# A GRU in front of an RK4 network: the GRU's input products made in one go in fp32 ahead of the first step

## The reference

```python
def cell(h, x):                       # layer 0, GRU; initial h = cond
    gi = x @ W_ih + b_ih              # the input products
    gh = h @ W_hh + b_hh
    i_r, i_z, i_n = jnp.split(gi, 3, axis=-1)
    h_r, h_z, h_n = jnp.split(gh, 3, axis=-1)
    r = jax.nn.sigmoid(i_r + h_r)
    z = jax.nn.sigmoid(i_z + h_z)
    n = jnp.tanh(i_n + r * h_n)
    h_new = (1.0 - z) * n + z * h
    return (h_new, h_new)
...
def _derivative(q, p, drive, coupling, bias):     # layer 1, four times a step
    i_couple = jnp.tanh(q) @ coupling.T
    dq = q - q ** 3 / 3.0 - p + drive + i_couple + bias
    dp = EPSILON * (q + ALPHA - BETA * p)
    return (dq, dp)
...
x = x + gru(cond, x, ...)
x = x + rk4(cond, cond, x, ...)
x = x + attention_norm(x, ...)
x = x + resample(x, cond)
```

## Time and profile before

| what | value |
|---|---|
| time, median of 3 runs (lowest, highest) | 3905.99 us (3901.99, 3906.72) |
| the profiled execution's own time | 3899.93 us |
| its span (first to last instruction) | 3897.7 us |
| busy PE / DVE / POOL / ACT | 3572.1 / 3071.1 / 2305.7 / 1730.2 us |
| instructions | 307,384 |
| granted PE clock, mean | 0.984 |

### The profile page before, as it was taken

One profiled execution on the slowest core, in us unless ns is written; L12 is line 12 of the kernel. 1 busy time (PEld: TensorE's weight loads), 2 busy tenths in 40 slices (PEclk: granted clock), 3 DMA queues, 4 the chain that ended last, 5 costly groups with the idle time before them and its releaser, 6 DMA issues.

```text
span 3897.7 us, 307384 instructions
## 1 busy us (share of the span) xinstructions
PE 3572.1 (92%) x127757; PEld 3388.6 (87%) x127757; DVE 3071.1 (79%) x19466; ACT 1730.2 (44%) x14974; POOL 2305.7 (59%) x8762
## 2 busy tenths in 40 slices
PE   3999989999999999999999999999999999999987
PEld 3999988899898988999988998899999999899963
DVE  7877877777787877877777787788877778777876
ACT  3444444444444444444444444444444444444443
POOL 0666656666666666666666666666666666666642
PEclk7999999999999999999999999999999999999998
DMA  4000000000000000000000000000000000000001
GB/s 163 5 5 5 5 5 5 5 5 5 5 6 5 5 5 5 5 5 5 5 5 5 5 5 5 5 5 5 6 5 5 5 5 5 5 5 5 6 4 43
DMA packets 9266, 39.61 MB, mean 10 GB/s; under 512 B 524, under 2 KB 568, under 8 KB 7736
## 3 DMA queue, kind: packets, MB, share of 16 engines
q1 hardware_dynamic: 7776, 19.92, 1.4%
q10 hardware_dynamic: 88, 0.02, 0.0%
HBM read 15.75 MB, written 4.19 MB: 5 GB/s over the span
## 4 chain that ended last, share of the span: by engine, by line
PE 67%; DVE 11%; issue 10%; ACT 7%; POOL 5%; DMA 1%; DVEq 0%; SPq 0%; ACTq 0%; POOLq 0%
PE psum L1115 34%; PE psum L1088 23%; PE psum L1073 9%; ACT tpart L514 3%; POOL term L401 2%; DVE psum L890 2%; POOL sums L405 2%; ACT tfull L516 2%; DVE gates L775 2%; DVE tpart L832 1%; PE psum L1220 1%; DVE gates L769 1%; ACT qhat L521 1%; DVE psum L878 1%; ACT rz L481 1%
## 5 line engine op out<-in xcount | busy, mean ns | idle before, releaser
L1115 PE MATMUL psum<-tpart,cpl 128*128 128x32 f16 x65536 | 2025.7, 176 | 99.6 <-issue 80.9
L1115 PEld LDWEIGHTS psum<-tpart,cpl 128*128 128x128 f16 x65536 | 1814.8, 96 | 170.0 <-issue 117.3
L1088 PE MATMUL psum<-hpart,whh 128*128 128x32 f16 x49344 | 1520.6, 176 | 72.7 <-issue 56.2
L1088 PEld LDWEIGHTS psum<-hpart,whh 128*128 128x128 f16 x49344 | 1372.2, 96 | 97.8 <-issue 83.8
L514 ACT ACTIVATE tpart<-psum 128x8 f16<-128x8 f32 x4096 | 703.7, 178 | 1179.8 <-DVE psum L890 1145.4
L890 DVE TENSOR_REDUCE psum<-psum 128x8 f32<-128x24 f32 x4096 | 726.2, 189 | 325.8 <-PE psum L1115 245.0
L832 DVE SCALAR_TENSOR_TENSOR tpart<-tfull,tpart 128x8 f16<-128x8 f32 x4098 | 717.1, 178 | 147.0 <-ACT tfull L516 11.6
L401 POOL TENSOR_TENSOR term<-coef,qhat 128x32 f32<-128x32 f32 (+1 forms) x1536 | 431.0, 281 | 552.4 <-ACT qhat L521 551.5
L516 ACT ACTIVATE tfull<-psum 128x8 f32<-128x8 f32 x4096 | 688.1, 175 | 0.0
L878 DVE SCALAR_TENSOR_TENSOR psum<-cub,sums 128x16 f32<-128x16 f32 x1536 | 309.6, 202 | 228.7 <-POOL sums L405 147.6
L405 POOL TENSOR_TENSOR sums<-sums,term 128x32 f32<-128x32 f32 (+1 forms) x1536 | 410.3, 267 | 120.3
(11 more groups left out here) (167 smaller groups left out, 3642.4 us busy)
## 6 DMA issues: line engine op xcount, KB each, us to landing
xrow<-in_x_dram SPq DMA_DIRECT2D x4, 1024.0 KB, 13.4
out_dram<-space SPq DMA_DIRECT2D x16, 256.0 KB, 2.0
space<-in_L_cond_W_hh_dram SPq DMA_DIRECT2D x1, 3072.0 KB, 10.5
wih<-in_L_cond_W_ih_dram SPq DMA_DIRECT2D x1, 3072.0 KB, 19.8
space<-in_L_cond_coupling_dram SPq DMA_DIRECT2D x1, 1024.0 KB, 12.6
xrow<-in_cond_dram SPq DMA_DIRECT2D x1, 1024.0 KB, 4.4
wih<-in_L_cond_Wk_dram SPq DMA_DIRECT2D x1, 1024.0 KB, 9.8
wih<-in_L_cond_Wo_dram SPq DMA_DIRECT2D x1, 1024.0 KB, 11.8
```

The lines of the kernel that those rows point to most:

```text
L1088: mm = pe.matmul(gate_out[part][:, :, :, col:col + B], whh[:, w, k, n * P:(n + 1) * P], copies_in(hpart[:, k, :, :]), start=(col == 0 and ...
L1115: mm = pe.matmul(stage_out[a][:, :, :, col:col + B], cpl[:, w, k, n * P:(n + 1) * P], copies_in(tpart[:, s % 2, k, :, :]), start=(col == 0 ...
```

## The change

The input products leave the steps. Ahead of the first step x is loaded by chunks of 128 time steps (all batches), transposed, and multiplied with the unsplit fp32 W_ih, 128 steps x 4 batches = 512 columns at a time: 4 chunks x 12 tiles x 4 feature groups = 192 fp32 matmuls into four PSUM banks. ACT adds the bias and writes them into `gi`, now 48 x 512 columns of `space`, which holds all 512 steps. The coupling is transposed within chunk 1, and PE waits there until DVE has split it. The split of x and W_ih, their scales, `xpart`, `wihp`, `gisum` and DVE's sums go away. UNROLL goes away; the last two steps have no GRU work. W_ih is loaded in three column parts, behind the first chunk of x and ahead of W_hh.

```diff
-        XC = UNROLL * B
-        xpart = sb("xpart", [P, 2, UNROLL * KB], fp16)
-        gisum = sb("gisum", [P, G3, XC])
-        gi = sb("gi", [P, G3, UNROLL, B])
+        space = sb("space", [P, 48 * D])
+        gi = space[:, :].rearrange("p (t n b) -> p t n b", n=G3, b=B)
...
+            load_x(0)
+            for j in range(3):
+                sp.dma_start(wih[:, :, j * D:(j + 1) * D],
+                             W_ih[:, j * D:(j + 1) * D].rearrange("(k p) n -> p k n", p=P)).then_inc(in_wih[j], 16)
             sp.dma_start(w_row, W_hh.rearrange("(k p) n -> p k n", p=P)).then_inc(in_whh, 16)
+            load_x(1)
             sp.dma_start(c_row, coupling.rearrange("(n p) k -> p n k", p=P)).then_inc(in_c, 16)
...
+            def keep_inputs(i, tiles):
+
+                for n in tiles:
+                    g = i * G3 + n
+                    act.wait_ge(gi_mm, g + 1)
+                    act.activation(gi[:, i * P:(i + 1) * P, n, :], gbank[g % 4].rearrange("p (t b) -> p t b", b=B),
+                                   ACT.Identity, bias=bias3[:, 2, n:n + 1]).then_inc(gi_ready, 1)
...
+            for i in range(CHUNKS):
+                if i == CHUNKS - 1:
+                    act.wait_ge(whh_ready, 1)
+                keep_inputs(i, range(0, 2 * K))
+                if i + 1 < CHUNKS:
+                    turn_x(i + 1)
+                keep_inputs(i, range(2 * K, G3))
+                if i == 0:
+                    act.wait_ge(scales_ready, 1)
+                    for k in range(K):
+                        act.activation(whh[:, 0, k, :], w_row[:, k, :], ACT.Identity, scale=scale[:, 0:1]).then_inc(w_hi, 1)
...
-            for b in range(B):
-                dve.wait_ge(xT_ready, K * (b + 1))
-                dve.tensor_reduce(amax[:, 4 + b:5 + b], xT[:, :, :, b], AX.XY, ALU.max,
-                                  apply_absolute_value=True).then_inc(amax_ready, 1)
...
+            dve.wait_ge(gi_ready, GROUPS)
             dve.tensor_copy(hn_base.rearrange("p (k b) -> p k b", b=B),
                             bias3[:, 3, 2 * K:3 * K].unsqueeze(2).broadcast_to([P, K, B])).then_inc(hn_base_ready, 1)
...
-                    if u == 0 and s == 1:
-                        sum_inputs(N, at(2 * UNROLL))
-                    if u == UNROLL - 1 and s == 1:
-                        sum_inputs(RZ, at(3 * UNROLL))
...
+            def input_products(i, tiles):
+
+                for n in tiles:
+                    g = i * G3 + n
+                    if i == 0 and n % K == 0:
+                        pe.wait_ge(in_wih[n // K], 16)
+                    if n == 0:
+                        pe.wait_ge(xT_ready, B * (i + 1))
+                    if g >= 4:
+                        pe.wait_ge(gi_ready, g - 3)
+                    for k in range(K):
+                        mm = pe.matmul(gbank[g % 4], wih[:, k, n * P:(n + 1) * P], xT[:, i * P:(i + 1) * P, k, :],
+                                       start=(k == 0), stop=(k == K - 1))
+                    mm.then_inc(gi_mm, 1)
...
+            turn_x(0)
+            for i in range(CHUNKS):
+                input_products(i, range(0, 2 * K))
+                if i == 1:
+                    pe.wait_ge(in_c, 16)
+                    pe.wait_ge(xT_ready, 2 * B)
                     for k in range(K):
+                        for n in range(K):
+                            mm = pe.transpose(bounce[k][:, n * P:(n + 1) * P], c_row[:, n, k * P:(k + 1) * P], ident[:, :])
+                        mm.then_inc(cturned, 1)
+                    pe.wait_ge(cpl_ready, 1)
+                if i + 1 < CHUNKS:
+                    turn_x(i + 1)
+                input_products(i, range(2 * K, G3))
...
-                    if s == 3:
-
-                        if u == 0:
-                            pe.wait_ge(x_parts, at(3 * UNROLL))
-                        pe.wait_ge(z_sum, gru)
-                        input_products(range(u * G3 // UNROLL, (u + 1) * G3 // UNROLL))
```

More of the change, by code:

```diff
@@ L257, in build @@
         cturned = sem("cturned")
[L259 to L262, removed]
+        gi_mm, gi_ready = sem("gi_mm"), sem("gi_ready")
+        scales_ready, w_hi = sem("scales_ready"), sem("w_hi")
         whh_ready = sem("whh_ready")
@@ L383, in _, with step @@
             start_sums(1)
-            def step(at, u):
-                now, tail = at(u + 1), at(u + 2)
+            def step(t):
+                now, tail = t + 1, t + 2
                 pool.wait_ge(q1_ready, now)
@@ L411, in step @@
                         pool.wait_ge(x1keep_ready, now)
[L412 to L421, removed]
+                        if tail <= T:
+                            next_drive(tail, now)
+                if tail <= T:
+                    start_sums(tail)
+            for t in range(T):
+                step(t)
+            pool.wait_ge(gi_mm, GROUPS)
             pool.memset(onerow[:, :], 1.0)
@@ L497, in _ @@
             for v in (1, 2):
-                gate_input(v, v - 1, v - 1 if v > 1 else None, group=UNROLL)
+                gate_input(v, v - 1 if v > 1 else None)
                 sigmoid_r(v)
@@ L506, in _, with step @@
                 act.activation(tfull[:, a * HC:(a + 1) * HC], first[:, a * HC:(a + 1) * HC], ACT.Tanh).then_inc(tanh0_ready, 1)
-            def step(at, u):
-                now, tail, gru = at(u + 1), at(u + 2), at(u + 3)
+            def step(t):
+                now, tail, gru = t + 1, t + 2, t + 3
                 for s in range(4):
@@ L527, in step @@
                                        scale=k_stage[s]).then_inc(sq_ready[0], 1)
-                        h_high(at(u + 4), gru)
-                    if s == 1:
-                        gate_input(gru, u, tail, group=at(2 * UNROLL) if u == 0 else None)
+                        if gru < T:
+                            h_high(gru + 1, gru)
+                    if s == 1 and gru <= T:
+                        gate_input(gru, tail)
                         sigmoid_r(gru)
-                    if s == 2:
+                    if s == 2 and gru <= T:
                         candidate(gru)
                         sigmoid_z(gru)
-            for t in range(0, T, UNROLL):
-                at = counts(t)
-                for u in range(UNROLL):
-                    step(at, u)
+            for t in range(T):
+                step(t)
             for k in range(2 * K):
@@ L729, in bias_inputs @@
-            def bias_inputs(part, v):
-                tiles = tiles_of[part]
-                dve.wait_ge(gi_summed[part], v)
-                ins = dve.scalar_tensor_tensor(gi[:, tiles, :, :].rearrange("p n t b -> p n (t b)"), gisum[:, tiles, :],
-                                         kapx[:, 1:2],
-                                         bias3[:, 2, tiles].unsqueeze(2).broadcast_to([P, tiles.stop - tiles.start, XC]),
-                                         ALU.mult, ALU.add)
-                if part == RZ:
-                    ins.then_inc(gi_ready, UNROLL)
@@ L853, in window @@
                                       ALU.min, ALU.add).then_inc(sqkept_ready, 1)
-                    if not first:
+                    if not first and gated_step:
                         h_low(gru)
@@ L1043, in _, with turn_x @@
             pe.wait_ge(ident_ready, 1)
-            def turn_x(b):
-                pe.wait_ge(in_x[b % 2], 16 * (b // 2 + 1))
-                for n in range(K):
-                    e = b * K + n
+            def turn_x(i):
+                pe.wait_ge(in_x[i % 2], 16 * (i // 2 + 1))
+                for b in range(B):
+                    e = i * B + b
                     if e >= 4:
@@ L1096, in _ @@
             pe.wait_ge(whh_ready, 1)
-            pe.wait_ge(wih_ready, 1)
-            pe.wait_ge(cpl_ready, 1)
-            pe.wait_ge(x_parts, UNROLL)
-            input_products(range(G3))
             for v in (1, 2):
@@ L1104, in _ @@
                     gates_mm(c)
-            pe.wait_ge(x_parts, 2 * UNROLL)
-            pe.wait_ge(z_sum, 2)
-            input_products(range(G3))
             def stage_products(s, ks, ns):
@@ L1120, in _, with step @@
             k_first, k_second = range(HK), range(HK, K)
-            def step(at, u):
-                now, tail, gru = at(u + 1), at(u + 2), at(u + 3)
+            def step(now, gru):
                 for s in range(4):
```

205 lines of the change are left out of this document (59 added, 146 removed).

## The result

The changed kernel takes 3841.6 us (median of 4 runs, 3840.4 to 3844.2) where the kernel before takes 3904.0 (4 runs, 3894.3 to 3906.7): a ratio of 0.9845, interval 0.9827 to 0.9864. Forecast were 3955 us, slower, with a range from 3897 to 4015. **The forecast is wrong in sign**, and its range misses the time by 55 us.

A forecast was written before the change was run, and what follows sets the result against it. A step was bound by PE work and chain, 6.75 us, plus 0.415 of block-end stops. Prologue +119.5 less 66.5 from the steps gave +53 us on 3,899.9, 3,953, stated as 3955 us; range 3897 to 4015.

The forecast's parts named there:

- The chain of 4.22 + 2.53 = 6.75 us: Least step: 4.22 us from first stage products to last gate products' start, then 2.53 through POOL, DVE, ACT to next step.
- the input products fill a hole: Behind stage 3, the 24 input products (0.60 us) end level with the chain, so removing them frees nothing by itself.
- the 128 matmuls between stops: In the loop, PE stops where a block of 256 instructions, 128 matmuls with weight loads, has not come yet.
- part 1: Input products leave the step: block ends cost 0.30 us a step instead of 0.415, step 7.05, a saving of 0.115.
- a stop of 0.45 us: PE's wait at an instruction block's end, taken at the small end of the 0.46 and 0.81 us seen before.
- S1, G1, S2, G2, S3: Sections of 32 matmuls in a step: S with a stage's number is its products, G the gate products behind that stage.
- The first rival: Fetches run on while PE idles behind stage 3: step falls to 6.75 us, about 3807 in all; 10%.
- The 4.02 us between two resumes: PE's timeline before the change, from 1011.01 to 1015.03: 128 matmuls, 4.02 us for 3.2 of issue.
- part 2: DVE loses the input products' sums, bias and splits of x: 0.015 us per step gained, at most 0.05.
- part 3: The prologue grows by making all input products ahead: first stage product at 211.2 us against 91.7, +119.5 us.
- the 4.3 us for a slow clock: In the prologue, eight fp32 records at the start and after a pause take 2.1 us more, twice: 4.3.
- S0: The first stage's products in a step, 32 matmuls; PE was to idle 0.7 us or more ahead of them.

The follow-up runs named there:

- e5: Changed kernel plus three unread fp16 matmuls of 512 columns behind stage 3 of every step but the last two: 3808.0 us, ratio to before 0.9677.
- e1: Changed kernel plus 24 unread matmuls of 32 columns behind stage 3 of every step but the last two: 4051.0 us, ratio to before 1.0262.
- e2: Changed kernel plus 48 unread matmuls of 32 columns behind stage 3 of a step: 4412.3 us, ratio to before 1.1178.
- e6: Changed kernel plus 12 unread matmuls of 32 columns behind stage 3 of a step: 3870.7 us, ratio to before 0.9839.
- e4: Changed kernel plus 16 small matmuls once ahead of the loop, moving all block ends by 16 matmuls: 3842.35 us, ratio to before 0.9734.
- e10: The changed kernel itself, repeated on another chip where the kernel before took 3917.1 us: 3841.9 us, ratio 0.9803.
- e7: Changed kernel, but only the first 32 time steps' products made ahead, the rest in 360 jobs of 16 time steps behind stage 3: 3703.5 us, 0.9410.
- e9: Changed kernel, input products spread in jobs of 32 time steps behind stage 3 of every second step, three unread 512-column matmuls in other steps: 3665.6 us, 0.9485.
- e3: Kernel before with 21 of the 24 input products of a step left out, DVE's work on them kept: 3725.2 us, ratio 0.9437.
- e12: The version of e9 repeated on the same chip as e10: 3685.1 us, ratio to before 0.9403.

## Why the prediction was wrong

**What bounds the kernel now: nearly right.** The chain of 4.22 + 2.53 = 6.75 us is confirmed: full-clock steps of the changed kernel have a median of 6.70. That the input products fill a hole held (e5 fills it with about as much PE time and loses nothing), and so did the 128 matmuls between stops.

**The step that failed is the price of the block ends in part 1**, "Sum 0.14 + 0.27 + 0.35 + 0.22 + 0.22 = 1.2 per four steps, 0.30 per step. The step becomes 6.75 + 0.30 = 7.05". It took a stop of 0.45 us from the kernel before, held it fixed, and asked at each place what stands ahead of it. But a stop has no length of its own: it is what a block's 3.7 us of supply exceed PE's work and waits since the last block end. Measured in the changed kernel, in the prediction's own places S1, G1, S2, G2, S3: 0, 0, 0.05, 0.04 and 0.12 us at an end, where 0.14, 0.27, 0.35, 0.22 and 0.22 were put. That is 0.05 a step against 0.30. The sign that was missed is one division, of the earlier trace rows by the earlier trace rows: 7.165 us over 1.94 blocks is 3.70 us, and e1, e2 and e6 gave 3.73, 3.75 and 3.72 with quite different idle times. At 1.75 blocks the supply needs 6.48 us, less than the chain, so most of the stops go, 713 of 820. The first rival, "the hole feeds the fetches", was this mechanism, with its condition (a block under 3.86 us), and got 10%. Its objection, that the hole is in one place, was right in kind, as the 107 stops left stand where it said, in S2 to S3, and wrong in size: a block that holds the hole lasts 4.1 to 4.5 us, one without it 3.4 to 3.5 in the mean, and no two without it follow each other. The 4.02 us between two resumes, one pair, was read as the time of a block; the mean was 3.70.

**The rival's 3807 against 3841.6.** It is 34 us short: the step is 6.827 and not 6.75. The chain's 6.70 at full clock is even shorter. In the changed kernel's trace the steps at full clock have a mean of 6.758, so the 282 with a fall of the clock cost 0.07 a step over all, 35 us; the prediction had kept the clock where it was. The other 0.06 above 6.70 are about the 0.05 of stops. e5, with the clock held at full, took 3808. The step stays near 6.82 as the two change places: e4 has a clock of 0.862, 68 stops (0.03 us a step) and full-clock steps of 6.734; e10 has 0.898, 135 stops (0.07) and 6.772. Why e10 has more stops stays open.

**Where supply and chain come close** (within some 0.1 us), the mean lies above both: e5 has 6.62 by supply and 6.70 by chain, and 6.766; e7, 6.74 and 6.70, and 6.85. The larger of two means leaves out that single blocks lack the idle time: e5 still has 134 stops at 839 ends. This is probably why e7 to e9 gained somewhat less than the larger bound.

**DVE's work, part 2:** forecast 0.015 a step, at most 0.05. e3's own trace gives 0.06, and e3 against e5 the same. In the trace of the kernel before, steps with and without the sums differ by only 0.04 (0.02 over all steps, not clear of noise), as the prediction had read; in e3, where the supply no longer decides, they differ by 0.11. By this estimate some 30 us of the change's gain are DVE's. The term was undersized, but it is not what turned the sign.

**The prologue, part 3:** forecast +119.5, measured +116.5. The products took 165.5 us against 164.7, transposes of one chunk 1.91 against 2.1, the wait for the coupling 4.65 against 4.3, the start of the products 14.15 against 13.9 (the terms given there, four transposes of 0.19 and four evictions of 0.89, make 4.3 and not 4.7, so part of this fit is luck). Only the 4.3 us for a slow clock were too much: five records from 14.15 took 2.38, and only the transposes after the wait for the coupling were slow, 3.30 instead of 1.91.

The Trainium skill's "Runtime: NRT & Kernel Launch", section "Instruction fetch mechanics", says that crossing into a block is mostly hidden. The trace disagrees in the kernel before, where PE issues matmuls of 32 columns at 25 ns, 3.2 us for a block that takes 3.7 to come, and mostly agrees in the changed kernel, whose step leaves 3.9 us for each: 107 of 820 block ends still have a stop. The same section gives PE a store of 2048 instructions, which is eight blocks. No run here shows blocks lying ready by the eight: in the changed kernel the stops come evenly from the start of the loop to its end, though the supply has 4% to spare, and in it as in e1, e2, e4, e5, e6 and e10 each stop ends 2.1 to 3.0 us behind the start of the newest packet. By this, idle time helps the next block or so and isn't saved up for later.

## What to carry to other kernels

Divide the step's time by the blocks of instructions that PE issues in it: if the quotient stays the same between versions with different numbers of matmuls and different idle time, the kernel is bound by the supply of instructions, and each matmul taken out is worth its share of a block, down to the chain and no further. (The runs took them out, or put them in, behind stage 3 alone.) Work that must stay is then cheapest as few wide instructions in a hole that the chain leaves: the same products, made ahead in the prologue, cost 116 us, and spread over the holes in wide pieces little: e9's steps are 6.771 us on one chip and 6.804 on another (e12), where e5's, which have no such job, are 6.766 on a third. A hole left empty can cost as well, by the clock. And engine work that costs nothing under one bound can cost once that bound is gone, as DVE's sums do in e3.

## What the runs showed of the hardware

- A block of PE's instructions (128 matmuls with their weight loads, 16.4 KB) took 3.70 to 3.75 us to come, at a step of 7.17 us as at one of 7.96: 2.5 from the start of the queue's newest packet to the end of a stop, 1.25 from there to the start of the next packet (e1, e2). The kernel that it bounds took 3864 to 3947 us in five groups of runs, the one that it doesn't 3841.6 to 3842.4 in three of them.
- That supply isn't stored far ahead: with 4% of it to spare, 107 of 820 block ends of the changed kernel still had stops, evenly over the loop, in the three sections farthest behind the hole.
- Some 0.7 us of idle PE ahead of S0 in a step of 6.8 us went with a granted clock of 0.85 to 0.90 over the execution (the changed kernel, e4, e10). In the changed kernel's trace it fell from the upper of its two levels (2.4 GHz) to the lower (1.2 GHz) and rose again 290 times; three wide matmuls in the hole gave 0.99. At the lower level these narrow matmuls stood 26.7 ns apart instead of 25.4, and a step that was half at the lower level took 6.85 us instead of 6.70. What a step wholly at the lower level costs is not shown.
- fp32 matmuls of 512 columns ran at full speed, 0.43 us a record, from the first on at 14.15 us.
